# Layer two's dense part block by block, the finish's last addition on GpSimd, loads apart, asserted waits

## What is computed

```python
# third layer; x is the layer norm of the running features; src, dst hold the self loops too
Vh = (x @ Wv + bv).reshape(N, H, O)
e = exp(alpha - m[dst]);  denom = segment_sum(e, dst)
attn = segment_sum(Vh[src] * (e / denom[dst]), dst)     # (2500, 256)
h = x + (attn @ Wo + bo)
h = batch_norm(h, bn1_g, bn1_b)                          # over all nodes, per feature
h2 = relu(h @ W1 + b1) @ W2 + b2
h = batch_norm(h + h2, bn2_g, bn2_b)
```

## Time and profile before

| | |
|---|---|
| median of three runs | 2401.42 us |
| lowest and highest | 2392.27 and 2405.89 us |
| span of the profiled execution | 2391.8 us |
| busy share PE, DVE, POOL, ACT | 73%, 73%, 57%, 27% |
| granted TensorE clock, mean | 0.875 |

### The profile page before, as it was taken

How to read it: one execution, slowest core, us unless ns; L and a number is a source line. 1 busy time by engine, 2 the same in 40 slices (tenths; PEclk the granted TensorE clock), 3 DMA queues, 4 the chain that set the end, 5 groups by cost and what they waited for, 6 DMA issues and landing times. The chain is left out here.

```text
span 2391.8 us, 37962 instructions
## 1 busy us (share of the span) xinstructions
PE 1734.4 (73%) x10655; PEld 1375.4 (58%) x10655; DVE 1746.7 (73%) x2746; ACT 635.2 (27%) x1452; POOL 1369.3 (57%) x1451
## 2 busy tenths in 40 slices
PE   4697036888665664999985999404688999758498
PEld 4476024566444452899974777403466666547387
DVE  6788735899555557555674888996599999786676
ACT  4364100000000004454521333104011111125464
POOL 4777777777777772000026777778777777700060
PEclk9799578999777887899997999856899999879799
DMA  5646645666333332000005666753466666430100
GB/s 157 211 150 215 203 125 159 211 209 194 105 106 106 105 102 71 1 2 19 1 31 188 212 207 209 246 185 117 145 215 217 211 213 200 125 105 1 44 10 35
DMA packets 119979, 321.05 MB, mean 134 GB/s; under 512 B 37105, under 2 KB 62985, under 8 KB 106339
## 3 DMA queue, kind: packets, MB, share of 16 engines
q0 software_dynamic: 62304, 170.45, 24.7%
q1 hardware_dynamic: 54239, 143.57, 17.1%
q10 hardware_dynamic: 3364, 6.16, 0.8%
HBM read 249.14 MB, written 70.96 MB: 134 GB/s over the span
## 5 line engine op out<-in xcount | busy, mean ns | idle before, releaser
L1397 DVE TENSOR_TENSOR ms_msg<-e_ring,ms_ps_w 128x1040 f32<-128x1040 f32 (+1 forms) x352 | 438.4, 1245 | 287.1 <-SPq L1340 284.2
L1414 PE MATMUL ms_ps_m<-ms_msg,ms_pick 128*128 128x260 f32 x1408 | 404.3, 444 | 210.0 <-DVE ms_msg L1397 125.5
L972 POOL DMA_INDIRECT e_ring<-table,e_index x465 | 445.0, 957 | 141.5 <-issue 137.4
L1414 PEld LDWEIGHTS ms_ps_m<-ms_msg,ms_pick 128*128 128x128 f32 x1408 | 301.0, 222 | 313.3 <-issue 260.6
L1414 PE MATMUL ms_ps_m<-ms_msg,all_xn 128*128 128x272 f32 x1408 | 382.0, 419 | 82.3 <-issue 55.7
L972 POOL DMA_INDIRECT e_ring<-table,l_index x369 | 359.4, 974 | 114.2 <-issue 110.7
L1414 PEld LDWEIGHTS ms_ps_m<-ms_msg,all_xn 128*128 128x128 f32 x1408 | 267.1, 199 | 197.1 <-issue 148.0
L847 PE MATMUL sc_ps_e<-sc_keys,sc_hot 125*128 125x100 bf16 (+1 forms) x3840 | 293.7, 230 | 22.3 <-DVE all_xn L792 19.6
L1014 POOL DMA_INDIRECT w_staged<-table,l_stage_index x256 | 262.1, 1024 | 81.6 <-issue 66.3
L847 PEld LDWEIGHTS sc_ps_e<-sc_keys,sc_hot 125*128 125x128 bf16 x3840 | 256.1, 98 | 71.7 <-DVE all_xn L792 25.1
L792 DVE TENSOR_REDUCE all_xn<-sc_ps_e 128x800 f32 (+1 forms) x240 | 235.5, 984 | 15.2 <-PE sc_ps_e L847 11.8
(11 more groups left out here) (463 smaller groups left out, 3029.2 us busy)
## 6 DMA issues: line engine op xcount, KB each, us to landing
ahead<-w_staged SPq DMA_DIRECT2D x32, 1056.0 KB, 4.5
e_ring<-ahead SPq DMA_DIRECT2D x32, 1056.0 KB, 5.1
ahead<-e_ring SPq DMA_DIRECT2D x20, 1040.0 KB, 4.4
e_ring<-ahead SPq DMA_DIRECT2D x20, 1040.0 KB, 5.1
e_ring<-table,e_index POOLq DMA_INDIRECT x465, 2.8
e_ring<-table,l_index POOLq DMA_INDIRECT x369, 2.8
w_staged<-L_ffn_w SPq DMA_DIRECT2D x2, 2048.0 KB
w_staged<-table,l_stage_index POOLq DMA_INDIRECT x256
```

Source lines behind the costliest of these rows:

```text
L972: pool.indirect_dma_start(out=g.ring[:, slot * QUAD + i // GT, i % GT, :], out_offset=None, in_=s.table[:, :], in_offset=bass.IndirectOffs ...
L1397: dve.tensor_tensor(msg[:, b, :, 0:R].rearrange("p t (h o) -> p t h o", h=H), ring[:, bass.ds(slot, 1), :, :].rearrange("p a t (h o) -> p ...
L1414: mm = pe.matmul(ps_m[b][:, 0:W], pick[:, b, t, :], msg[:, b, t, :], start=t == 0, stop=t == GT - 1)
```

## The change

Six things are done.

1. In the dense part each engine's program up to the first batch norm goes block by block: shares, turning, high and low parts, base and projection of neighbouring blocks alternate. The banks in PSUM are dealt anew (three for the attention, two for the base, two for the projection, one that holds `inv` and `loop` for all blocks).
2. POOL makes the addition of the two shares into `attn`.
3. w.o is the second load on SP, w.w1 and w.w2 have a semaphore of their own, and ACT issues the seven columns, ahead of its Exp.
4. `mid` lies in `xn` instead of in `acc`.
5. POOL clears fewer semaphores in the dense part; SP clears the others (`s.spent`) ahead of its load in the second message loop.
6. Register values that are used in waits are checked at run time: `steps_through` on POOL and SP, the group on DVE.

```diff
@@ def steps_through @@
     _, (steps,) = nc.values_load_multi_w_load_instructions(
-        s.release[0:1, bass.ds(quad, 1)], engines=[engine], min_val=0, max_val=NS, skip_runtime_bounds_check_because=STEPS_BOUND)
-    return steps
+        s.release[0:1, bass.ds(quad, 1)], engines=[engine])
+    return nc.s_assert_within(steps, 0, NS)
@@ def step_values: the group of DVE alone is checked @@
-            return [nc.s_assert_within(v, 0, top, skip_runtime_bounds_check_because=STEPS_BOUND) for v, top in zip(values, tops)]
+            return [nc.s_assert_within(v, 0, top) if held else nc.s_assert_within(v, 0, top, skip_runtime_bounds_check_because=STEPS_BOUND)
+                    for v, top, held in zip(values, tops, waited)]
@@ pass_messages, sync @@
                 sp.wait_ge(between.back_copied, backs)
+                for sem in s.spent:
+                    sp.sem_clear(sem)
@@ transformer_dense @@
-        mid = acc[:, :, :].rearrange("p a w -> p (a w)")[:, 0:KB * NP].rearrange("p (k n) -> p k n", k=KB)
+        mid = s.xn[:, :, :].rearrange("p a d -> p (a d)").rearrange("p (b k t) -> p b k t", b=NB, k=KB)
...
+        held_bank = ps[7]
+        inv_held, loop_held = (held_bank[:, i * NT * H:(i + 1) * NT * H].rearrange("p (a h) -> p a h", h=H) for i in range(2))
...
+                for b in range(NB):
+                    tiles = slice(b * SUB, (b + 1) * SUB)
+                    pool.wait_ge(scaled, b + 1)
+                    pool.wait_ge(owned, b + 1)
+                    pool.tensor_tensor(attn[:, tiles, :].rearrange("p a (h o) -> p a h o", h=H), v[:, tiles, :, 0:O],
+                                       acc[:, :, 0:D + H].rearrange("p a (h o) -> p a h o", h=H)[:, tiles, :, 0:O], ALU.add).then_inc(attn_ready, 1)
...
+                shares(0)
+                shares(1)
+                low_weight(0)
+                low_turned(0)
+                shares(2)
+                dve.wait_ge(columns_in, 16 * len(loads[3:]))
+                for b in range(1, NB):
+                    if b + 2 < NB:
+                        shares(b + 2)
+                    low_turned(b)
+                    projected(b - 1)
+                    if b == NB - 2:
+                        low_weight(1)
+                projected(NB - 1)
+                low_weight(2)
                 batch_norm(0, mid, w.bn1_g[:, :], w.bn1_b[:, :], low_normed)
@@ scalar @@
+                for dst, src in loads[3:]:
+                    act.dma_start(dst, src, allow_slow_non_contiguous=True).then_inc(columns_in, 16)
                 act.wait_ge(loop_shifted, 1)
                 act.activation(loop[:, :, :], loop[:, :, :], ACT.Exp).then_inc(loop_ready, 1)
-                act.wait_ge(loaded, 16 * len(loads))
...
+                for b in range(NB):
+                    for kb in range(KB):
+                        act.wait_ge(turned, b * KB + kb + 1)
+                        high_part(act, in_high[:, kb, block_cols(b)], turn_bank(b, kb)[:, :]).then_inc(copied, 1)
+                    if b >= 1:
+                        bases(b - 1)
...
@@ tensor @@
+                turn_base(0)
+                for b in range(NB):
+                    turn_attention(b)
+                    if b >= 1:
+                        turn_base(b)
+                        if b == 1:
+                            pe.wait_ge(weight_lows, 1)
+                        project(b - 1)
+                project(NB - 1)
```

More of the change, by code:

```diff
@@ L1990, in _ @@
                 link(dve.reciprocal(inv[:, :, :], inv[:, :, :]))
-                link(dve.tensor_tensor(loop[:, :, :], loop[:, :, :], inv[:, :, :], ALU.mult))
+                dve.tensor_copy(inv_held, inv[:, :, :]).then_inc(held, 1)
+                dve.tensor_tensor(loop_held, loop[:, :, :], inv[:, :, :], ALU.mult).then_inc(held, 1)
+                dve.wait_ge(held, 2)
                 def low_weight(i):
@@ L2002, in _ @@
                     dve.wait_ge(v_in[b], 16)
[L2003 to L2012, removed]
@@ new lines, in statistics, with projected @@
+                def statistics(b, d):
+                    dve.bn_stats(stats[:, d, b, :], mid[:, b, d, 0:min((b + 1) * TB, N) - b * TB]).then_inc(stats_ready, 1)
+                def projected(b):
+                    for d in range(KB):
+                        i = b * KB + d
+                        dve.wait_ge(proj_ready, i + 1)
+                        dve.wait_ge(base_copied, i + 1)
+                        dve.scalar_tensor_tensor(out=mid[:, b, d, :], in0=proj_bank(d)[:, :], scalar=w.bo[:, d:d + 1], in1=mid[:, b, d, :],
+                                                 op0=ALU.add, op1=ALU.add).then_inc(proj_added, 1)
+                    for d in range(KB):
+                        dve.wait_ge(proj_added, b * KB + d + 1)
+                        statistics(b, d)
@@ L2062, in node_statistics @@
                         dve.bn_stats(s.node_stats[:, a, :], s.x[:, a, :])
-                for i in range(NB * KB):
-                    b, d = i // KB, i % KB
-                    dve.wait_ge(proj_ready, i + 1)
-                    dve.wait_ge(base_copied, i + 1)
-                    dve.scalar_tensor_tensor(out=mid[:, d, block_cols(b)], in0=ps[4 + i % 4][:, :], scalar=w.bo[:, d:d + 1], in1=mid[:, d, block_cols(b)],
-                                             op0=ALU.add, op1=ALU.add).then_inc(proj_added, 1)
-                    dve.wait_ge(proj_added, i + 1)
-                    statistics(b, d)
-                dve.wait_ge(proj_added, NB * KB)
-                dve.wait_ge(loaded, 16 * len(loads))
+                shares(0)
[13 more added lines that the diff above has]
+                low_weight(2)
                 batch_norm(0, mid, w.bn1_g[:, :], w.bn1_b[:, :], low_normed)
@@ new lines, in project @@
+                def project(b):
+                    pe.wait_ge(lows_ready, (b + 1) * KB)
+                    for d in range(KB):
+                        if b >= 1:
+                            pe.wait_ge(proj_added, (b - 1) * KB + d + 1)
+                        cols = slice(d * P, (d + 1) * P)
+                        split_products(pe, proj_bank(d)[:, :], [((o_high[:, kb, cols], o_low[:, kb, cols]), (in_high[:, kb, block_cols(b)], in_low[:, kb, block_cols(b)]))
+                                                                for kb in range(KB)]).then_inc(proj_ready, 1)
```

111 lines of the change are left out of this document (59 added, 52 removed).

## The result

The changed kernel takes 2409.01 us in the median of 20 runs (2401.86 to 2415.04); the kernel before took 2401.49 in the 20 runs beside them (2389.58 to 2406.01). The ratio is 1.0034, with a 95% interval of 1.0019 to 1.0048. The prediction was 2401, no change. Both profiled executions lie near the low end of their runs: spans of 2391.8 us before and 2402.2 after.

The account below looks back on a forecast made before the run. DVE's step and POOL's beat were taken to bound the loops by turns; the dense part's possible 11 us went to start, low part and PE's chain, leaving -0.3, checks 0. Set on the median: 2401 us, range 2389 to 2418.

Parts of the forecast that it names:

- What bounds the kernel: Message loops: DVE's step of 2.16 us and POOL's gather beat of 1.25 us take turns; the dense part was read separately.
- The start: Dense part: seven column loads on ACT ahead of its Exp delay DVE's first share by 4.2 us, bounds +2 and +6.
- POOL's addition: Dense part: POOL's 128x1024 addition of the two shares takes 2.5 us, bounds 0.73 and 4.7.
- The clock and the chain: Dense part: PE works through the blocks in sequence, at half clock until the first projection ends at 2133.8, then fast.
- Rival C: Dense part: PE stays at 1.2 GHz, so each block's cycle becomes 10.7 us; +17 us, chance 0.12.
- PE's cycle: Dense part: each further block costs PE 5.9 us at the fast clock, including a hole of 1.3.
- The exposed low part: Dense part: the low part of w.w2 now stands right ahead of the batch norm and costs 1.2 us.
- rival A: The forecast itself: PE's cycle at the fast clock bounds the dense part; -0.3 us, -5 to +4, chance 0.55.
- Costed at nothing: Side effects taken as hidden, among them SP's 45 semaphore clears ahead of its xn load, 2.8 us if uncovered.
- The asserted waits: Message loops: checks behind step loads on DVE, POOL and SP add 0.1 to 0.4 each, hidden: 0, bounds to 144 us.
- The prediction's own sign: Message loops: the prediction called itself wrong if a loop's length moved by 10 us.
- Rival D: Message loops: the checks are not hidden; +15 us through POOL's loads, +138 if they held DVE's sequencer; chance 0.16.

Follow-up runs that it names:

- 1: The kernel before with all the run-time checks (part six of the change) and nothing else: 2411.14 us, ratio 1.0039.
- 3: The kernel before with a maximum with 0 on each waited value in place of a check: 2401.70 us, ratio 1.0005.
- 6: The kernel before with checks on DVE alone, a maximum with 0 on POOL and SP, on a slow chip: ratio 1.0087.
- 9: The kernel before with checks on DVE alone, a maximum with 0 on POOL and SP, on another slow chip: ratio 1.0107.
- 13: The kernel before with checks on DVE alone, a maximum with 0 on POOL and SP, where before takes 2408.64 us: 2412.65 us, ratio 1.0037.
- 5: The kernel before with checks on POOL alone, a maximum with 0 on SP and DVE, on a slow chip: ratio 0.9989.
- 10: The kernel before with checks on POOL alone, a maximum with 0 on SP and DVE, on another slow chip: ratio 1.0015.
- 14: The kernel before with checks on POOL alone, a maximum with 0 on SP and DVE, where before takes 2408.64 us: 2406.96 us, ratio 1.0010.

## Why the prediction was wrong

- **What bounds the kernel**: right for the two limits within a loop. Wrong is that POOL's gathers keep 1.25 us "whatever the others do": beside DVE's one-hots they take up to 1.2 us instead of 0.95 and up to 9.7 in the stages after. Left out is that POOL's work from the staging on is one chain to the loop's end, so the stage of the edge scores should have been read too.
- **The start**, +4.2: mis-sized, measured 6.69 against 4.11 us before from the part's start to the first share, +2.6. Seven issues took 4.1 us, not 5.5, the last 0.58.
- **POOL's addition**, 2.5: measured 2.57 (5.15 for two) and 2.40. The Trainium skill, GPSIMD Engine Reference, section Specifications, on two SBUF inputs of VectorE, pointed to this one and not to 4.7.
- **The clock and the chain**: the clock was 0.50 up to 2143.2 and 1.00 from there. The products go from 0.43 to 0.23 us apart at 2143.2, within the first projection, 23.5 us after the part's start; the forecast was 2134, 26.8 after it. The first projection's last product ends 24.2 us after the start, forecast 26.6; 1.6 of the 2.4 is the start. By the Trainium skill, TensorE: Matmul & The Clock Gate, section What's actually happening, activity releases the throttle; with a hole of 1.2 to 1.3 us in each cycle it stayed released. Rival C didn't come.
- **PE's cycle**, 5.9: measured 5.95 and 5.99. **The exposed low part**, 1.2: measured 1.13. The sum for the dense part was -0.3; measured -2.7, all of the difference gone by the end of the first projection. The mechanism was rival A.
- **Costed at nothing**: SP's load of xn starts at 1649.28 instead of 1645.30, behind 46 clears of 3.1 us, and the first message product at 1658.8 instead of 1658.0. The clears are covered, as forecast.
- **The asserted waits, 0**: this step failed. The argument "so 0.1 to 0.4 more is hidden" is right where it was made: a check takes 0.21 us on DVE, 0.17 on POOL, and neither loop's step moved. But it costed the checks only in the steps that they stand in. The runs show 0.37 to 0.39%, 9 us, in place of 0, and none that can be told without DVE's checks; the profiles point to 7.5 us of it beside the edge scores, where POOL's gathers fall into step with DVE's one-hots. The prediction's own sign came: the second loop is 11 us longer, while its step is the same, because the rows arrive later. Rival D had the sign; its two prices, +15 by POOL's loads and +138 by DVE's, were for other mechanisms, and POOL's checks cost nothing.

Shown: that having the checks on DVE is the cause (1 against 3, 6, 9 and 13 against 5, 10 and 14). Made likely by the table: where the time goes. Open: whether on the chips of 2400 to 2409 us the checks cost by running or by moving the score stage 40 instructions on, and how they reach a stage without a check. The holes of 0.4 us at L792 come with them and would bring DVE to the even cycle in which the gathers are hit; that they do is argued, not shown, and so is what delays the instructions.

A version under both: the new dense part with clamps and the columns behind the Exp, 0.9979, 0.9963 and 0.9997 on three chips: 5, 10 and 1 us, which only one of the three intervals clearly tells from none.

## What to carry to other kernels

A sequencer that is a step ahead hides an instruction in that step, but this doesn't price it: find the engine whose work is one chain over several stages, and ask of every stage in it who slows it or shares its beat. A maximum with 0 on a value before a wait cost nothing that could be told here, a check on DVE 9 us; but the maximum bounds from below alone and added no instruction on DVE. Put loads behind the small operation that another engine waits for, even where they are needed soon.

## What the hardware showed unexpectedly

**Two engines in step.** A gather of 0.95 us takes 1.20 when it starts with DVE's 125x1024 bf16 comparison; since 2.75 us is then the cycle of both, the coincidence holds itself up for many cycles: 65 of 147 gathers were slow so in experiment 1, 17 of 156 in the kernel before.

**A gather held for twelve instructions.** POOL and then DVE in experiment 1:

```profile
1606.01 9.73 POOL L1014 DMA_INDIRECT w_staged<-table,l_stage_index  x1 [0.30 <-issue]
```

```profile
1606.02 3.01 DVE L1224 SCALAR_TENSOR_TENSOR all_xn<-all_xn 128x640 f32<-128x640 f32 x4
1608.96 3.02 DVE L1224 SCALAR_TENSOR_TENSOR all_acc<-all_acc 128x640 f32<-128x640 f32 x4
1611.90 3.02 DVE L1225 TENSOR_TENSOR all_acc<-all_acc,all_xn 128x640 f32<-128x640 f32 x4
```

The gather ends 0.8 us after the last of twelve instructions of 0.75. In the kernel before, gathers beside the same twelve passed, 1.16 us each, and one was held 8.57 us by the next twelve:

```profile
1610.51 1.17 POOL L1014 DMA_INDIRECT w_staged<-table,l_stage_index  x1 [0.30 <-issue]
...
1625.04 8.57 POOL L972 DMA_INDIRECT e_ring<-table,l_index  x1 [0.30 <-issue]
```

The Trainium skill, SBUF — State Buffer, section SBUF: two separate sides, has the lock last one instruction; here a gather waits for twelve, in some executions only. That it is this lock is not shown.

**Chips differ.** The same kernel took 2400 and 2409 us on two chips and 2749 to 2775 on three others, with the same durations of its instructions and more holes without a wait; an edit that costs 0.4% on the one kind costs 0.9 to 1.4% on the other.
